# Six changes of order on four engines of a fused two-layer kernel (Trainium2, one core)

## The chip, the cores and the metric

One NeuronCore of a Trainium2 chip runs the whole kernel in one launch. The metric is the device time of one execution in microseconds (us); lower is better. The engines run side by side, each one through its own list of instructions in the order in which that list was written: TensorE (PE, matmuls, with its weight loads as PEld), VectorE (DVE), ScalarE (ACT), GpSimd (POOL) and SyncE (SP, which here only starts transfers). They wait for each other at semaphores. An instruction that waits holds up everything behind it on its engine.

## The reference

The input `x` has 4 batches of 1024 tokens with 1024 features. Four blocks follow, each with a residual and a layer norm:

```
x = layernorm(x + x @ (W0 * block_mask).T)                 # 32x32 block mask
x = layernorm(x + x @ W1.T + bias + lora(x, adapter of the batch))
x = layernorm(x + small_model(x))                          # 1024 -> 128, 4 layers, 128 -> 1024
x = layernorm(x + x @ W.T + b + routed rank-16 experts)
```

A layer of the small model is: layer norm, silu, a complex exponential scan along the sequence, residual, layer norm, 128 to 512 with silu, 512 to 128, residual. Everything is float32. The kernel gets that accuracy by splitting each factor into a high and a low part and adding three products (hi·hi, hi·lo, lo·hi).

## The kernel before, in words

The 4096 tokens are 32 tiles of 128. The first dense block works on tiles s = 0 to 31, the second on s = 32 to 63 (`A_END` = 32, `B_END` = 64), then the small model runs on 8 units of 512 tokens for each layer, and the last dense block takes s = 64 to 95. A tile has 8 chunks of features (`KC`) and two halves of 512 output columns. A product of one tile and one half is 8 chunks by 3 matmuls (`terms`), of 128x512 each.

**The pair stage.** Tiles 7 to 26 go in ten pairs p = 0 to 9 through seven half-size products in place of eight (a Strassen-like scheme). On PE they stand in the order A11, A12, S2, S3, S1, S4, A22 (`paired_product`), 12 matmuls each. ACT makes the high parts (`op_hi`), DVE the sums of x (`add_x`) and the low parts (`op_lo`). ACT copies three results from PSUM to SBUF (`hold(p, 0..2)`, for A11, S2 and S1) and DVE adds them to others (`join(p, 0..3)`). A22 of a pair waits for `join(p, 1)`, which needs `hold(p, 2)`. S1 waits for `hold(p, 1)`. After a tile's rows are joined, DVE takes the statistics (`aggregate`), POOL the reciprocal root (`root`), and ACT normalises the row (`normalise`: a small `shift`, L1410, and the row, L1413). POOL takes the row apart into two planes of 16 bits (`part_planes`), and ACT starts their transfer to a scratch tensor in device memory (`send_planes`).

**The second dense block.** Its input comes from that scratch tensor by transposing DMAs on SP's queue (`load_x`, L632, two for a tile, into `x_planes`). POOL puts the planes together into `x_in` (`join_planes`, L2640), and ACT and DVE split it into high and low (`split_x`). `x_planes` and `x_in` are one buffer each, so tile s+1 can't be fetched before tile s is joined, and not be joined before tile s is split. In tiles 27 to 31 the weights of the second block are built as well: a product on PE (`weight_part`, L979), a sum on DVE (`weight_sum`, L1932), high and low parts. `split_x(32)` stands ahead of the sums for parts 13 to 15 on both ACT and DVE.

**The last eight tiles of it (s = 56 to 63)** also carry the set-up of the small model. DVE builds tables of angles and centres weights (`prepare(j)` with j = s - 56); PE turns each finished row (`turn_y`, L1030), ACT and DVE split it (`split_y`), and a projection (`project_pair`) takes two tiles at a time to 128 features. From s = 60 on the small model's first steps begin (`EARLY` = 4): ACT squares a unit (`square1`, L1502), PE takes the variance (`variance1`, L1072), DVE copies it (`take_var1`), POOL takes the root (`root1`, L2653, turn letter "a"), PE spreads it (`spread_rstd1`, L1078), DVE scales (`scale1`), ACT applies silu (`silu_x`, L1513), then come rotation and scan. The second half of a tile's product waits until DVE has taken the tile before out of its bank (L1840).

All orders are written out by hand, in one long sequence for each engine; there is no scheduler.

Of the kernel before, what the change touches and what calls it, by code (L numbers as in the profile page):

```python
# [9 lines left out]
BATCHES = 4  # L10
# [13 lines left out]
FIRST = 3  # L24
# [15 lines left out]
A_END, B_END, D_END = TILES, 2 * TILES, 3 * TILES  # L40
# [7 lines left out]
EARLY = 4  # L48
# [194 lines left out]
def build(nc, a, out):  # L243
# [184 lines left out]
    with ExitStack() as ctx:  # L428
# [175 lines left out]
        def _(sp):  # L604
# [123 lines left out]
            for s in range(2, A_END):  # L728
# [11 lines left out]
                if s == S_END:  # L740
                    for n in range(2, 6):
                        load_w(n)
                    sp.wait_ge(mm_done, product_count(PAIRS - 1, A22))
                    sp.dma_start(a_in[:], a["expert_a"]).then_inc(lora_loaded, 16)
                    load_x(s + 3)
                if s > S_END:
                    for n in range(TAIL_PARTS[s].start + 3, min(TAIL_PARTS[s].stop + 3, PARTS)):
                        load_w(n)
                if s == S_END + 2:
                    for i in range(2):  # L750
                        sp.wait_ge(stored[(S_END - 1 - i) % 2], 16 * ((S_END - 1 - i) // 2 + 1))
                    sp.dma_start(bias1[:], a["bias1"].partition_broadcast(P)).then_inc(bias_loaded, 16)
                if s + 2 >= A_END:
                    load_x(s + 2)

            for s in range(A_END, B_END):
                b, j = batch_of(s), s % TPB
# [588 lines left out]
        def _(act):  # L1346
# [45 lines left out]
            def t_hi(m):  # L1392

                act.wait_ge(summed, KC + 1 + 2 * m + 2)
                if m >= 4:
                    act.wait_ge(w0_lo_ready, t_count(m - 2))
                act.activation(t_place(m)[:, 0], t_source(m), ACT.Identity).then_inc(w0_hi_ready, 1)
# [215 lines left out]
            normalise(3)  # L1613
            evacuate(4, 1)
            t_hi(7)
            send_planes(3)
            split_x(FIRST + 3)
            normalise(4)
            evacuate(5, 0)
            for j in range(A11, S1):  # L1620
                op_hi(0, j)
            send_planes(4)
            evacuate(5, 1)
            normalise(5)
            evacuate(6, 0)
            evacuate(6, 1)
# [3 lines left out]
            for p in range(PAIRS):  # L1630
# [6 lines left out]
                    op_hi(p + 1, A11)  # L1637
                if p > 0:
                    send_planes(a - 2)
                normalise(a - 1)  # L1640
                if more:
                    op_hi(p + 1, A12)
                else:
                    split_x(S_END)
                hold(p, 1)
                if more:
                    op_hi(p + 1, S2)
                    op_hi(p + 1, S3)
# [33 lines left out]
            for s in range(A_END, B_END):  # L1682
# [17 lines left out]
                    weight_hi(n + 1)  # L1700
                if s == A_END:
                    send_planes(s - 1)
                if s > B_END - EARLY:
                    silu_x(s - 1 - B_END + EARLY)
                if s >= B_END - EARLY:
                    square1(s - B_END + EARLY)
                if i >= 1:
                    split_y(s - 1)

# [60 lines left out]
        def _(dve):  # L1770
# [688 lines left out]
            for s in range(A_END, B_END):  # L2459
# [23 lines left out]
                if b + 1 < BATCHES:  # L2483
                    for m in range(n, n + 2):
                        weight_sum(m)
                        weight_lo(m)
                if i >= 1:
                    split_y(s - 1)
                if b + 1 == BATCHES:
                    prepare(j)  # L2490
                if s >= B_END - EARLY:
                    turn = s - B_END + EARLY
# [116 lines left out]
        def _(pool):  # L2609
# [137 lines left out]
            root(S_END - 1)  # L2747
            part_planes(S_END - 2)
            for s in range(S_END, A_END):
                for i, n in enumerate(TAIL_PARTS[s]):  # L2750
                    if n % 2:
                        weight_lo(n)
                    if i == 1 and s > S_END:
                        root(s - 1)
                part_planes(s - 1)
                if s + 2 >= A_END:
                    join_planes(s + 2)

            order = [("d", rotate_back(0)), ("d", rotate_back(1)), ("b", rotate), ("a", root1), ("e", root2)]
            root(A_END - 1)  # L2760
            part_planes(A_END - 1)
            for s in range(A_END, B_END):
                if s + 2 < B_END:
                    join_planes(s + 2)
                root(s)
                if B_END - EARLY <= s + 1 < B_END:
                    turn_of(order, s + 1 - B_END + EARLY)

# [87 lines left out]
```

## Time and profile before

| | before |
|---|---|
| time, median of 3 runs | 1662.61 us (1660.96 to 1665.57) |
| the profiled execution | 1665.42 us, span 1663.4 us |
| PE busy | 1617.6 us, 97% |
| DVE, ACT, POOL busy | 1171.7, 667.3, 615.5 us (70%, 40%, 37%) |
| mean granted TensorE clock | 0.989 |

The span is the time from the first to the last instruction; the execution's own time has about 2 us around it. PE is busy nearly all the time, so what a change of order can give lies in the time in which PE stands still, and in the time after it in which PE runs at a lower clock. PE busy is a share of modelled matmul times and hides this second part; it is seen in the granted clock of a stretch. In a row of the timeline, the bracket at the end is the idle time of that engine just before the instruction and what ended it.

### The profile page before, as it was taken

The page shows a single profiled execution, that of the slowest core. Times are in us where ns is not written, and L with a number is a line of the kernel's source. Part 1 is how long each engine was busy: PE and PEld are TensorE (multiplying, and loading weights), DVE is VectorE, ACT ScalarE, POOL GpSimd, SP SyncE. Part 2 cuts the span into 40 slices and gives each one's busy share as a digit, 9 for nine tenths or more (in the row PEclk, how much of TensorE's full clock was granted, in tenths as well). Part 3 has the DMA queues.
Part 4 walks back from the last instruction along what each step waited for, and adds up shares of the span by engine and source line. Part 5 has one row for each costly group of instructions (what it writes and reads, how often), then busy time and mean ns, then how long its engine had stood idle before and what let it go on. Part 6 is the DMA issues. An engine that isn't in the chain of part 4 may idle for free.

```text
span 1663.4 us, 22807 instructions
## 1 busy us (share of the span) xinstructions
PE 1617.6 (97%) x7734; PEld 1298.9 (78%) x7734; DVE 1171.7 (70%) x2150; ACT 667.3 (40%) x987; POOL 615.5 (37%) x507
## 2 busy tenths in 40 slices
PE   9999999999999999998899999999899999999998
PEld 7877777878888888887776676666688788888886
DVE  7878887646656565675777777778867777776633
ACT  3544444433333333322345555545533333333311
POOL 4324333443333222221477777772213212221200
PEclk9999999999999999999989999999999999999999
DMA  7233333544545444632140000002546555555421
GB/s 279 84 113 121 114 101 127 170 114 132 126 111 125 113 122 116 162 92 76 42 161 26 1 1 1 1 13 95 206 146 214 192 198 190 187 195 188 134 82 51
DMA packets 140195, 196.58 MB, mean 118 GB/s; under 512 B 75954, under 2 KB 84146, under 8 KB 139826
## 3 DMA queue, kind: packets, MB, share of 16 engines
q1 hardware_dynamic: 115250, 125.92, 25.9%
q10 hardware_dynamic: 24832, 69.22, 10.8%
q8 instruction: 63, 1.03, 0.3%
q14 instruction: 50, 0.41, 0.1%
HBM read 105.97 MB, written 72.35 MB: 107 GB/s over the span
## 4 chain that ended last, share of the span: by engine, by line
PE 75%; DVE 10%; issue 7%; POOL 3%; ACT 3%; DMA 2%; ACTq 0%; SPq 0%; POOLq 0%; DVEq 0%
PE ps L884 14%; PE ps L886 13%; PE ps L885 13%; PE ps L1130 6%; PE ps L1072 3%; PE ps L963 2%; PE ps L965 2%; PE ps L964 2%; PE ps L1030 2%; PE ps L1120 2%; PE ps L1078 2%; PE ps L1122 2%; PE ps L1121 2%; PE ps L896 2%; PE ps L1098 1%
## 5 line engine op out<-in xcount | busy, mean ns | idle before, releaser
L2622 POOL TENSOR_TENSOR rstd<-var_eps,minus_half 128x1 f32<-128x1 f32 x96 | 87.5, 911 | 562.1 <-DVE minus_mean L1908 561.9
L884 PE MATMUL ps<-wall_x,x_hi 128*128 128x512 f32 x688 | 277.0, 403 | 8.9 <-ACT wall_x L1475 3.1
L885 PE MATMUL ps<-wall_x,x_hi 128*128 128x512 f32 x688 | 271.4, 394 | 0.0
L886 PE MATMUL ps<-wall_x,x_lo 128*128 128x512 f32 x688 | 270.9, 394 | 0.0
L884 PE MATMUL ps<-wall_y,x_hi 128*128 128x512 f32 x512 | 201.9, 394 | 0.0
L885 PE MATMUL ps<-wall_y,x_hi 128*128 128x512 f32 x512 | 199.4, 389 | 0.0
L886 PE MATMUL ps<-wall_y,x_lo 128*128 128x512 f32 x512 | 199.4, 389 | 0.0
L884 PEld LDWEIGHTS ps<-wall_x,x_hi 128*128 128x128 f32 x688 | 131.1, 191 | 39.7 <-issue 5.4
L886 PEld LDWEIGHTS ps<-wall_x,x_lo 128*128 128x128 f32 x688 | 131.2, 191 | 28.6
L885 PEld LDWEIGHTS ps<-wall_x,x_hi 128*128 128x128 f32 x688 | 131.3, 191 | 25.6
L1840 DVE TENSOR_TENSOR row<-ps,bias 128x512 f32<-128x512 f32 x128 | 87.8, 686 | 86.7 <-PE ps L886 85.4
L1541 ACT ACTIVATE g<-ps,b 128x512 f32<-128x512 f32 x128 | 83.9, 679 | 123.8 <-PE ps L1122 123.4
L1130 PE MATMUL ps<-g,w 128*128 128x512 f32 x256 | 126.9, 619 | 0.0
L1843 DVE BATCH_NORM_STATS2 stats<-row 128x6 f32<-128x512 f32 x152 | 105.1, 694 | 28.8 <-ACT row L1403 24.3
L1410 ACT ACTIVATE shift<-minus_mean,rstd 128x1 f32<-128x1 f32 x96 | 28.0, 292 | 239.5 <-POOL rstd L2622 239.5
L1413 ACT ACTIVATE row<-row,shift,rstd 128x1024 f32<-128x1024 f32 x96 | 119.5, 1245 | 3.2
L886 PEld LDWEIGHTS ps<-wall_y,x_lo 128*128 128x128 f32 x512 | 96.1, 188 | 20.4
L885 PEld LDWEIGHTS ps<-wall_y,x_hi 128*128 128x128 f32 x512 | 96.2, 188 | 18.9
L884 PEld LDWEIGHTS ps<-wall_y,x_hi 128*128 128x128 f32 x512 | 96.2, 188 | 18.8
L2640 POOL COPY x_in<-x_planes 128x1024 uint16<-128x1024 uint16 x64 | 85.2, 1378 | 26.8 <-DMA x_planes<-x_scratch 26.8
L1369 ACT ACTIVATE x_hi<-ps 128x1024 fp32r<-128x1024 f32 x32 | 32.7, 1023 | 150.6 <-PE ps L896 147.6
L1072 PEld LDWEIGHTS ps<-mean_col,squares 128*128 128x128 f32 x520 | 68.1, 194 | 26.2 <-issue 12.0
(329 smaller groups left out, 3619.2 us busy)
## 6 DMA issues: line engine op xcount, KB each, us to landing
x_scratch<-row ACTq DMA_DIRECT2D x32, 512.0 KB, 2.7
x_in<-x_scratch SPq DMA_DIRECT2D x32, 512.0 KB, 3.9
out<-row ACTq DMA_DIRECT2D x32, 512.0 KB, 2.7
x_in<-in_x_t SPq DMA_DIRECT2D x29, 512.0 KB, 3.5
w_first<-in_w_t SPq DMA_DIRECT2D x56, 256.0 KB, 3.0
x_scratch<-planes_early ACTq DMA_DIRECT2D x27, 512.0 KB, 3.1
cx<-x_scratch SPq DMA_DIRECT2D x24, 512.0 KB, 4.2
x_scratch<-cx ACTq DMA_DIRECT2D x24, 512.0 KB, 3.6
```

Source lines behind the costliest of these rows:

```text
L884: pe.matmul(bank, hi[:, k], wall[:, k, 0, cols], start=(k == 0), stop=False)
L885: pe.matmul(bank, hi[:, k], wall[:, k, 1, cols], start=False, stop=False)
L886: return pe.matmul(bank, lo[:, k], wall[:, k, 0, cols], start=False, stop=(k == KC - 1))
L896: last = pe.transpose(ps_x[:, k * P:(k + 1) * P], x_in[s % 2][:, k * P:(k + 1) * P], ident[:])
L1072: last = pe.matmul(ps[:, bank, c:c + 1], squares[:, c * P:(c + 1) * P], mean_col[:], start=True, stop=True)
L1130: pe.matmul(ps[:, OUT], w2[:, FCH * (n // UNITS) + i], g[:, i], start=(i == 0), stop=(i == FCH - 1)).then_inc(o_done, 1)
L1413: act.activation(row[:, i], row[:, i], ACT.Identity, bias=shift[:, i:i + 1], scale=rstd[:, i:i + 1])\
L1541: act.activation(g[:, i], ps[:, F0 + i % 2], ACT.Silu, bias=of_layer(b1[:, :, i], n))\
L1840: dve.tensor_tensor(row[:, i, cols], ps[:, out_bank(s, half)], bias[:, cols], ALU.add)\
L1843: mark(dve.bn_stats(stats[:, i, half], row[:, i, cols]))
L2622: pool.tensor_tensor(rstd[:, i:i + 1], var_eps[:, i:i + 1], minus_half[:, 0:1], ALU.pow)\
L2640: pool.tensor_copy(halves[:, part], x_planes[:, part].rearrange("p k t -> p (k t)"))\
```

## The change

No instruction is added or taken away; the list of PE is the same. Six things move:

1. SP and POOL, tile 32: its two transposing DMAs are issued ahead of the loads of weight parts 13 to 15, and `join_planes(32)` comes ahead of the work of tile 30 on POOL.
2. ACT, start: `split_x(6)` ahead of `send_planes(3)`, and `evacuate(5, 1)` ahead of `send_planes(4)`.
3. ACT, each of the ten pairs: `hold(p, 1)` ahead of `normalise(a - 1)` and of what follows it.
4. ACT, tiles 61 to 63: `square1` ahead of `silu_x`.
5. DVE, tiles 59 to 62 (j = 3 to 6): `prepare(j)` ahead of `split_y(s - 1)`.
6. POOL, from tile 33 on: `join_planes(s + 3)` right behind `root(s)`; so it stands ahead of the small-model steps of the turn.

```diff
@@ SP
+                if s + 2 == A_END:
+                    load_x(A_END)
                 if s > S_END:
                     for n in range(TAIL_PARTS[s].start + 3, min(TAIL_PARTS[s].stop + 3, PARTS)):
                         load_w(n)
...
-                if s + 2 >= A_END:
-                    load_x(s + 2)
+            load_x(A_END + 1)
@@ ACT, start
+            split_x(FIRST + 3)
             send_planes(3)
-            split_x(FIRST + 3)
...
+            evacuate(5, 1)
             send_planes(4)
-            evacuate(5, 1)
@@ ACT, pairs
                 if p > 0:
                     send_planes(a - 2)
+                hold(p, 1)
                 normalise(a - 1)
                 if more:
                     op_hi(p + 1, A12)
                 else:
                     split_x(S_END)
-                hold(p, 1)
@@ ACT, last tiles of the second block
+                if s >= B_END - EARLY:
+                    square1(s - B_END + EARLY)
                 if s > B_END - EARLY:
                     silu_x(s - 1 - B_END + EARLY)
-                if s >= B_END - EARLY:
-                    square1(s - B_END + EARLY)
@@ DVE
+                if b + 1 == BATCHES and j >= 3:
+                    prepare(j)
                 if i >= 1:
                     split_y(s - 1)
-                if b + 1 == BATCHES:
+                if b + 1 == BATCHES and j < 3:
                     prepare(j)
@@ POOL
             for s in range(S_END, A_END):
+                if s + 2 == A_END:
+                    join_planes(A_END)
...
-                if s + 2 >= A_END:
-                    join_planes(s + 2)
+            join_planes(A_END + 1)
...
+            join_planes(A_END + 2)
             for s in range(A_END, B_END):
-                if s + 2 < B_END:
-                    join_planes(s + 2)
                 root(s)
+                if s + 3 < B_END:
+                    join_planes(s + 3)
                 if B_END - EARLY <= s + 1 < B_END:
                     turn_of(order, s + 1 - B_END + EARLY)
```

ACT in pair 2, before. `held` are the copies of A11 and then S2; the two `x_hi` are the high parts of A11 and A12 for pair 3; `shift` and `row` are the normalising of tile 10:

```order
L1390 ACTIVATE held<-ps 128x512 [waits evac_dve,mm_done]
L1383 ACTIVATE x_hi<-x_in_126 128x512 [waits mm_done,x_loaded1]
L1421 DMA x_scratch<-planes_early 128x2x1024 [waits parted]
L1410 ACTIVATE shift<-minus_mean,rstd 128x1 [waits rstd_ready,ve_ready]
L1413 ACTIVATE row<-row,shift,rstd 128x1024 [waits shift_ready]
L1383 ACTIVATE x_hi<-x_in_126 128x512 [waits mm_done,x_loaded1]
L1390 ACTIVATE held<-ps 128x512 [waits evac_dve,mm_done]
L1383 ACTIVATE sum_hi<-x_sum 128x512 [waits mm_done,x_summed] x2
```

The same place after the change (line numbers there are one higher):

```order
L1391 ACTIVATE held<-ps 128x512 [waits evac_dve,mm_done]
L1384 ACTIVATE x_hi<-x_in_126 128x512 [waits mm_done,x_loaded1]
L1422 DMA x_scratch<-planes_early 128x2x1024 [waits parted]
L1391 ACTIVATE held<-ps 128x512 [waits evac_dve,mm_done]
L1411 ACTIVATE shift<-minus_mean,rstd 128x1 [waits rstd_ready,ve_ready]
L1414 ACTIVATE row<-row,shift,rstd 128x1024 [waits shift_ready]
L1384 ACTIVATE x_hi<-x_in_126 128x512 [waits mm_done,x_loaded1]
L1384 ACTIVATE sum_hi<-x_sum 128x512 [waits mm_done,x_summed] x2
```

The copy of S2, with its wait for PE, has moved ahead of the normalising and of the high part of A12.

DVE in tile 59, before. `row` and `stats` are the first half of tile 59, `y_lo` is `split_y(58)`, then comes `prepare(3)` (from `b_68` to `table`), then the second half of tile 59:

```order
L1843 BN_STATS stats<-row 128x6 [waits evac_dve]
L1947 TENSOR_TENSOR y_lo<-ps,y_hi 128x8x128 [waits y_hi_ready]
L2073 TENSOR_TENSOR b_68<-ps,b_in 128x16 [waits bias_done,mlp_loaded]
L2060 TENSOR_SCALAR cross_wide<-table,anchor 128x512
...
L2066 SCALAR_TENSOR_TENSOR table<-table,anchor,cross_wide 128x512 x3
L1840 TENSOR_TENSOR row<-ps,bias_142 128x512 [waits stored1,mm_done,dve_done]
```

After the change:

```order
L1844 BN_STATS stats<-row 128x6 [waits evac_dve]
L2074 TENSOR_TENSOR b_68<-ps,b_in 128x16 [waits bias_done,mlp_loaded]
L2061 TENSOR_SCALAR cross_wide<-table,anchor 128x512
...
L2067 SCALAR_TENSOR_TENSOR table<-table,anchor,cross_wide 128x512 x3
L1948 TENSOR_TENSOR y_lo<-ps,y_hi 128x8x128 [waits y_hi_ready,dve_done]
L1841 TENSOR_TENSOR row<-ps,bias_142 128x512 [waits stored1,mm_done]
```

The wait for ACT's high part of y now stands behind the table work.

POOL at tiles 59 to 61, before. `x_in_126` from `x_planes` is `join_planes` (61, then 62), `rstd` is `root`, `rstd_97` is `root1`, `x_rot_178` is the first rotation:

```order
L2640 COPY x_in_126<-x_planes 128x1024 [waits lo_ready,x_loaded0]
L2640 COPY x_in_126<-x_planes 128x1024
L2622 TENSOR_TENSOR rstd<-var_eps,minus_half 128x1 [waits normed,ve_ready]
L2653 TENSOR_TENSOR rstd_97<-var_95,minus_half 128x4 [waits var1_ready]
L2640 COPY x_in_126<-x_planes 128x1024 [waits lo_ready,x_loaded0]
L2640 COPY x_in_126<-x_planes 128x1024
L2622 TENSOR_TENSOR rstd<-var_eps,minus_half 128x1 [waits normed,ve_ready]
```

After the change:

```order
L2643 COPY x_in_126<-x_planes 128x1024 [waits lo_ready,x_loaded0]
L2643 COPY x_in_126<-x_planes 128x1024
L2625 TENSOR_TENSOR rstd<-var_eps,minus_half 128x1 [waits normed,ve_ready]
L2643 COPY x_in_126<-x_planes 128x1024 [waits lo_ready,x_loaded0]
L2643 COPY x_in_126<-x_planes 128x1024
L2656 TENSOR_TENSOR rstd_97<-var_95,minus_half 128x4 [waits var1_ready]
L2625 TENSOR_TENSOR rstd<-var_eps,minus_half 128x1 [waits normed,ve_ready]
```

The join of tile 62 no longer stands behind `root1(0)`.

## Rows read from the trace of the kernel before

**Rows 1.** Waits of PE: line and tile, releaser, us in total, times, longest.
```profile
PE ps L1072 <- ACT squares L1502: 6.0, 3, 2.8
PE ps L963 <- ACT held L1390: 5.1, 5, 1.6
PE ps L1078 <- POOL rstd L2653: 2.4, 3, 1.1
```

**Rows 2.** Stretches: length, busy us of PE, PEld, DVE, ACT, POOL; PE clock, DMA share, GB/s.
```profile
349.00:358.00 9.00, 5.78 (x19) 4.36 (x18) 5.87 (x9) 4.86 (x7) 2.72 (x4) 0.81 0.45 117
756.00:764.00 8.00, 5.93 (x20) 4.67 (x20) 5.58 (x11) 2.17 (x3) 1.52 (x1) 0.79 0.09 34
781.00:791.00 10.00, 7.16 (x34) 5.73 (x33) 4.60 (x8) 3.87 (x5) 1.27 (x1) 0.83 0.36 111
800.00:808.00 8.00, 5.96 (x28) 5.08 (x27) 6.25 (x6) 2.36 (x3) 1.33 (x1) 0.79 0.16 66
245.00:254.00 9.00, 7.28 (x32) 5.43 (x31) 7.64 (x11) 5.21 (x9) 2.48 (x2) 1.00 0.27 80
```

**Rows 3.** Timeline at tile 32: start, length, engine, line, what, idle before.
```profile
329.56 0.38 SPq L752 DMA_DIRECT2D bias<-in_bias  x1
340.58 11.18 SPq L632 DMA_TRANSPOSE x_planes<-x_scratch  x4
346.53 0.14 DVE L1908 TENSOR_SCALAR minus_mean<-mean_var 128x1 f32<-128x1 f32 x1
346.55 2.60 POOL L2640 COPY x_in<-x_planes 128x1024 uint16<-128x1024 uint16 x2 [2.22 <-DMA x_planes<-x_scratch]
350.27 1.23 DVE L1823 TENSOR_TENSOR x_lo<-x_in,x_hi 128x1024 fp32r<-128x1024 f32 x1 [3.60 <-ACT x_hi L1369]
352.57 0.67 PE L979 MATMUL ps<-b_rows,a_rows 128*128 128x512 f32 x1 [3.22 <-DVE w_first L1932]
```

**Rows 4.** Timeline of tiles 59 to 61.
```profile
751.68 1.22 DVE L1947 TENSOR_TENSOR y_lo<-ps,y_hi 128x1024 fp32r<-128x1024 f32 x1 [4.09 <-ACT y_hi L1481]
757.38 0.69 DVE L1840 TENSOR_TENSOR row<-ps,bias 128x512 f32<-128x512 f32 x1
758.12 0.50 PE L884 MATMUL ps<-wall_x,x_hi 128*128 128x512 f32 x1 [2.07 <-DVE row L1840]
774.17 1.02 POOL L2653 TENSOR_TENSOR rstd<-var,minus_half 128x4 f32<-128x4 f32 x1 [13.34 <-DVE var L2120]
775.13 2.60 POOL L2640 COPY x_in<-x_planes 128x1024 uint16<-128x1024 uint16 x2
777.77 1.06 ACT L1369 ACTIVATE x_hi<-x_in 128x1024 fp32r<-128x1024 f32 x1 [9.50 <-POOL x_in L2640]
802.62 1.34 PE L1072 MATMUL ps<-mean_col,squares 128*128 128x1 f32 x8 [2.04 <-ACT squares L1502]
```

**Rows 5.** Timeline of the start.
```profile
84.39 0.47 PE L884 MATMUL ps<-wall_x,x_hi 128*128 128x512 f32 x1 [1.57 <-issue]
```

**Rows 6.** Timeline of pairs 2 and 5, by engine.
```profile
143.05 0.29 ACT L1410 ACTIVATE shift<-minus_mean,rstd 128x1 f32<-128x1 f32 x1 [2.35 <-POOL rstd L2622]
144.49 0.39 PE L963 MATMUL ps<-wall_y,sum_hi 128*128 128x512 f32 x1
196.17 0.39 PE L963 MATMUL ps<-wall_x,x_hi 128*128 128x512 f32 x1
196.37 0.60 ACT L1390 ACTIVATE held<-ps 128x512 f32<-128x512 f32 x1 [0.33 <-PE ps L965]
198.89 0.39 PE L963 MATMUL ps<-wall_y,sum_hi 128*128 128x512 f32 x1
202.96 0.29 ACT L1410 ACTIVATE shift<-minus_mean,rstd 128x1 f32<-128x1 f32 x1 [5.46 <-POOL rstd L2622]
210.66 0.69 DVE L1893 TENSOR_TENSOR row<-ps,held 128x512 f32<-128x512 f32 x1
211.50 0.47 PE L963 MATMUL ps<-wall_y,x_hi 128*128 128x512 f32 x1
```

## The prediction, made blind

> **What bounds the kernel now.** I read the page's busy shares first: PE works 97% of the span, so the time is the matmuls' own time, the stops of PE, and the slow stretches of its clock. Next the list of PE's waits [rows 1]: no wait is large, and three lines touched by the change stand in it. L1072 waits for ACT's squares (6.0 us in three stops), L963 for a held block (5.1 us in five, the longest 1.6), and L1078 for the root `rstd` (2.4 us in three, the longest 1.1). Two more stand in the timelines: 3.22 us at tile 32 [rows 3] and 2.07 us at tile 59 [rows 4].
>
> Then I read the granted clock around these stops [rows 2]. In 349 to 358, after the stop of 3.22, it is 0.81, in 756 to 764 (a stop of 2.07) 0.79, in 781 to 791 (2.8, the longest of L1072) 0.83, and in 800 to 808 (2.04) 0.79. The level between the ends can only be a mixture of 2.4 and 1.2 GHz, so the missing share is time lost: 9 × 0.19 = 1.71, 8 × 0.21 = 1.68, 10 × 0.17 = 1.70, 8 × 0.21 = 1.68. Every stop of 2.04 us or more thus costs 1.7 us beyond itself. In 245 to 254, which holds a stop of 1.6 us for a held block, the clock stays at 1.00. Where the price begins between 1.6 and 2.04 us these rows don't tell.
>
> **Tile 32 (part 1 of the change).** The transposes are issued at 340.58 and the join begins at 346.55, 5.97 us later [rows 3]. After the change they stand behind the bias load, whose issue is at 329.56, ahead of three weight loads. Issued at about 330 they have landed at about 336; the data that they fetch was sent tiles before. The join of 2.60 us then runs about 336.6 to 339.2, seven microseconds early. What is late next is not the join but DVE: its statistics stand ahead of its part of the split and end at 346.53 + 0.14 = 346.67. So `x_lo` can go from 350.27 to about 346.7 and, with it, the sum behind it on which PE stopped: 3.5 us, against a stop of 3.22. It goes whole, with a margin of only 0.3 us, and its slow stretch with it: 3.22 + 1.7 = **−4.9 us**. POOL does the join in an idle time and its other work starts at most half a microsecond late; the three weight loads leave SP about 1 us later and are needed a tile or more later. Both I cost at nothing; uncovered, each is at most its own delay, 1 us. If the transposes gain nothing, this term is 0; if only the stop shrinks below 2 us, it is about −1.7 − 1.2.
>
> **Tiles 59 to 63 (parts 4 to 6).** At tile 59 DVE is idle for 4.09 us until ACT's high part of y is there, and starts `y_lo` at 751.68; then `prepare(3)` runs, and the second half row comes at 757.38 for 0.69, for which PE waits till 758.12 [rows 4]. `y_lo` takes 1.22, so the table work is 757.38 − 751.68 − 1.22 = 4.5 us long. With `prepare(3)` ahead it fills the 4.09 of idleness, ends about 752.2, `y_lo` follows to 753.4 and the row comes at about 754 rather than 757.4. The stop of 2.07 goes with its slow stretch: −3.8. The price is `y_lo` some half to one microsecond late; the projection that needs it is a tile away. At tile 60 POOL idles 13.34 us in front of the first unit's root, because that root waits for DVE's copy of the variance, and the join of tile 62 stands behind it, at 775.13. ACT's high part of tile 62 therefore waits 9.50 us, till 777.77. After the change the join stands behind `root(59)`, and can run about 18 us earlier; ACT's split comes ten or more earlier, and everything behind it on ACT, the squares of the second unit above all, is no longer late. Further the squares stand ahead of the silu and its table load (part 4). So I take the 2.8 us stop of L1072 as gone with its slow stretch (−4.5), the 1.1 at L1078 (−1.1) and the 2.04 at 802.62 with its slow stretch (−3.7). The sum is 3.8 + 4.5 + 1.1 + 3.7 = **−13.1 us**. What can be late next is `split_y`, now behind the table work: 4.5 us of work moved ahead of it against 4.09 of idleness leaves half a microsecond of lateness at tile 59; where DVE has less idleness, at most the full 4.5 late. The bounds of this term are 0 (all becomes other waits) and −15.
>
> **Start (part 2).** The stop of 1.57 us at 84.39 has "issue" for its releaser [rows 5]; the high parts it really waits for stand on ACT behind a transfer's start, itself waiting for POOL. The change takes them out of that queue. But the next A22 products wait for DVE's chain below, so of 1.57 us I keep only about 0.35 by pair 1; 0 to 1.6 are the bounds.
>
> **Pairs (part 3).** The held block is now ahead of the normalising on ACT. Before, at pair 5, the normalising starts at 202.96, as soon as POOL's root is there, and the copy comes after it. A product is 198.89 − 196.17 = 2.72 us on PE [rows 6], and a copy starts 0.20 after the next product's first matmul (196.37 − 196.17) and takes 0.60. So from now on the normalising, N, can't start before S3's start + 0.80. What follows N sets A22: shift, row, the high part of A12, DVE's low parts and sums and `join(p, 1)` at 210.66, then A22 at 211.50: 211.50 − 202.96 = 8.54 us. From S3's start to A22 PE itself needs three products, 8.16 us. A22 thus waits 0.80 + 8.54 − 8.16 = 1.18 us in a pair that had no wait, and a pair takes 7 × 2.72 + 1.18 = 20.22 us in place of 19.04. In pair 2, N was at 143.05 and S3 at 144.49. Less 0.35 from the start, plus 0.80, N comes at 144.94: 1.9 late. Between there and pair 5's N the trace has 59.91 us for three pairs, 19.97 each, since there were waits already. If pair 5's intervals become 20.22 flat, the lateness grows by 0.75 only; if each grows by the full 1.18, by 3.5. That gives 2.6 to 5.4 us at pair 5; I take 4.2, and no more after it, since there the held block was waited for already. That wait (5.1 us in all) goes from the list but gains nothing: S1 starts earlier, and A22 still waits for the 8.54 us chain from N. It moves from S1 to A22, and there the two waits meet: 1.18 plus up to 1.6 is 2.8 us in one piece, above the 2.04 after which the clock was seen to fall. I take two such falls of 1.7. The term is 4.2 + 3.4 = **+7.6 us**. Below, it can be −5 (the waits of 5.1 just go); above, see the third rival.
>
> **Sum.** −4.9 − 13.1 + 7.6 = −10.4 us. The profiled execution took 1665.42 us, 2.1 us of it around the span of 1663.4; −10.4 makes 1655.0. It lay 2.8 us above the median of 1662.61, to which the same step gives 1652.2. I forecast **1652 us**. A difference below 0.3%, 5 us, can't be told from no change here.
>
> **Rivals.**
> *The held block costs nothing.* If the chain behind N has slack that I don't see (DVE's row work could be started by an earlier root), A22 keeps its time and the first gains stay: −4.9 − 13.1 and a little of the start, up to −1.6: 1643 to 1645 us. For it: most pairs show no wait of PE at S1, and the wait list has 5.1 us to gain. Against it: 8.54 > 8.16 in pair 5. Chance 26%.
>
> *The released waits only change their name.* In tiles 59 to 63 the late `split_y` (up to 4.5 us) and the late DVE work behind it take the place of the roots and squares; half of 13.1 comes back, and the pair term stays: −4.9 − 6.5 + 7.6 = −3.8, 1659 us. For it: DVE is busy 70% of the time and 6.25 of 8 us in 800 to 808 [rows 2]; against it: it had 4.09 idle at tile 59. Chance 14%. Of this kind, that the transposes at tile 32 land late because the change of SP's queue doesn't bring them forward: −13.1 + 7.6 = −5.5, 1657 us; chance 5%, as 5.97 us from issue to join leaves ten microseconds of room.
>
> *The clock falls in every pair (the other side).* The merged or lengthened wait at A22 need only be a little longer than I have it (above about 2 us instead of 1.18) for a slow stretch in each pair. A pair then takes 20.22 + 1.7 = 21.9 us against 19.97, times nine intervals, 17.6, and 1.9 from the first: +19.5 − 18.0 = +1.5, 1664 us; with waits of 2 us in each, 8 more, 1672 us. It decides if the wait at A22 passes the 1.6 to 2.04 us between which the fall begins. Chance 8%. Here the Trainium skill speaks against the change: "TensorE: Matmul & The Clock Gate", section "HAM oscillation — how this bites in real kernels", says that waits that come back between bursts of matmuls throw the clock back to half in each tile anew. By that rule alone this rival's 1664 would be the forecast; the trace before agrees only for stops of 2.04 us and more, and its 1.6 us stops in the pairs left the clock at 1.00.
>
> **How the numbers follow.** My forecast 47%, the held block free 26%, half the tail gain 14%, transposes late 5%, clock in every pair 8%. The range: downward to the first rival with half a microsecond, 1642.5; upward through 1657 and 1659 to 1660; beyond it lies the last rival and the rest of the scatter. Faster by over 0.3% (below 1657.6): the forecast, the first rival and part of the others, 0.81; within 0.3%: 0.13; slower: 0.06.
>
> **What would show it.** In the list of waits: the held block at L963 near 0 and about 10 us for DVE's row or `x_hi` at L963 new; no stop over 2 us at tile 32, nor before 758, 784 and 802; L1072's 6.0 down to about 1. In the timeline: the join of tile 32 seven, of tile 62 eighteen us earlier in its tile; N in the pairs 0.80 behind S3's start. In the windows: 1.00 at tiles 32 and 59 to 62, and two places below 1.00 in the pairs. The forecast is wrong if the time from tile 7 to tile 26 does not grow, or if the tail's waits return as waits for `y_lo` or the angle tables.

## The result, and the profile after

| | before | after |
|---|---|---|
| median of 5 runs | 1665.57 us (1660.96 to 1668.10) | 1655.73 us (1653.47 to 1656.24) |
| the profiled execution's span | 1663.4 us | 1654.3 us |
| PE busy | 1617.6 us | 1614.8 us |

The ratio is 0.9942 with a 95% interval of 0.9922 to 0.9962: 9.8 us faster between the medians of the same chip, where the forecast had 10.4. The median of 1655.73 lies inside the forecast's range of 1642.5 to 1660 and 3.7 us above its 1652. Of these, 3.0 are no error of a step: the forecast counted down from the earlier median of 1662.61, and the runs made beside the changed kernel put the kernel before at 1665.57.

To see where the time went, I take fixed points of the program in both timelines: the normalising of tiles 7, 26, 57 and 65 (the ACT instruction `shift`), and PE's first stop for squares of the next layer (at 890.70 us before, 878.88 after). The table gives how much each stretch grew against before. The first stretch contains the launch and the first loads; its length differs by up to 2 us either way between executions (−2.1 to +1.8 in the table of the experiments).

| stretch | growth | forecast |
|---|---|---|
| launch to tile 7 (start, most of pair 0) | +1.0 | in the pairs' term |
| tile 7 to 26 (pairs) | +7.0 | +7.6 |
| 26 to 57 (tile 32) | −5.0 | −4.9 |
| 57 to the stop at 890.70 | −14.9 | −13.1 |
| from there to tile 65 (small model) | +2.9 | 0 |

PE's waits in the changed kernel, in the columns of [rows 1]; line numbers are one to three higher:

```profile
PE ps L964 <- DVE row L1894: 12.1, 9, 2.3
PE ps L1073 <- ACT squares L1503: 1.1, 1, 1.1
PE ps L999 <- ACT b_rows L1438: 0.9, 1, 0.9
PE ps L1079 <- POOL rstd L2656: 0.8, 2, 0.6
PE ps L980 <- DVE w_first L1933: 0.7, 1, 0.7
PE ps L885 <- DVE row L1841: 0.7, 2, 0.5
```

The 5.1 us for a held block are gone, and nine waits of the same product family for a joined row, 12.1 us, stand in their place. The squares went from 6.0 to 1.1 us. A stop of 0.9 us for `b_rows`, at the end of the pairs, is new and I had not foreseen it.

The windows, in the columns of [rows 2]: the first three are the places of tile 32 and of tiles 59 to 61 in this run's time, the other three hold the A22 stops of pairs 1, 5 and 7.

```profile
357.00:366.00 9.00, 9.00 (x41) 7.38 (x41) 5.28 (x10) 4.70 (x8) 5.98 (x6) 1.00 0.17 59
759.00:767.00 8.00, 8.00 (x46) 6.88 (x45) 7.93 (x13) 3.18 (x5) 4.32 (x3) 1.00 0.36 110
773.00:783.00 10.00, 10.00 (x61) 8.82 (x61) 4.74 (x7) 4.91 (x7) 2.86 (x3) 1.00 0.26 93
130.00:140.00 10.00, 7.79 (x28) 5.96 (x27) 9.66 (x28) 5.08 (x8) 1.05 (x2) 0.83 0.47 159
216.00:225.00 9.00, 6.67 (x30) 5.45 (x30) 8.40 (x26) 4.93 (x9) 1.81 (x3) 1.00 0.36 117
258.00:267.00 9.00, 7.00 (x31) 5.74 (x31) 8.52 (x30) 4.51 (x9) 2.13 (x3) 1.00 0.39 120
```

The first three are the places of three of the stops in [rows 2]. PE is now busy for all of each stretch, at full clock. In the pairs one window, at 130 to 140, shows 0.83: 10 × 0.17 = 1.7 us lost. I had expected two of those.

Timeline of pair 4 in the changed kernel, beside [rows 6]; start, length, engine, line, what:

```profile
187.57 0.39 PE L964 MATMUL ps<-wall_y,sum_hi 128*128 128x512 f32 x1
187.77 0.60 ACT L1391 ACTIVATE held<-ps 128x512 f32<-128x512 f32 x1 [4.02 <-PE ps L966]
188.26 0.28 ACT L1411 ACTIVATE shift<-minus_mean,rstd 128x1 f32<-128x1 f32 x1
189.73 0.61 ACT L1384 ACTIVATE x_hi<-x_in 128x512 fp32r<-128x512 f32 x1
190.38 1.09 DVE L1851 TENSOR_TENSOR x_lo<-x_in,x_hi 128x512 fp32r<-128x512 f32 x1 [3.47 <-ACT x_hi L1384]
195.97 0.69 DVE L1894 TENSOR_TENSOR row<-ps,held 128x512 f32<-128x512 f32 x1
196.80 0.47 PE L964 MATMUL ps<-wall_y,x_hi 128*128 128x512 f32 x1 [0.91 <-DVE row L1894]
```

This is the chain that the prediction described. S3 starts at 187.57, the copy 0.20 later, the normalising 0.49 after that: 0.69 behind S3's start, where I had 0.80. From the normalising to A22 it is 196.80 − 188.26 = 8.54 us, the same as before. The idle time of DVE is the new thing here: it waits 3.47 us for the high part of A12, which stands behind the copy and the normalising on ACT.

In pair 5, one of the three with a long stop, the copy is not what the normalising waits for. The copy starts at 208.00 and takes 0.60; the normalising comes 2.1 us behind S3's start, with POOL's root:

```profile
209.91 0.29 ACT L1411 ACTIVATE shift<-minus_mean,rstd 128x1 f32<-128x1 f32 x1 [1.31 <-POOL rstd L2625]
```

From it to A22 at 218.44 it is again 8.53 us. The normalising waits for the later of the two, the copy or the root.

Timeline at tile 32, beside [rows 3]:

```profile
338.10 4.03 SPq L632 DMA_TRANSPOSE x_planes<-x_scratch  x2
344.69 2.66 POOL L2643 COPY x_in<-x_planes 128x1024 uint16<-128x1024 uint16 x2 [2.96 <-DVE x_lo L1824]
354.86 1.23 DVE L1824 TENSOR_TENSOR x_lo<-x_in,x_hi 128x1024 fp32r<-128x1024 f32 x1
355.69 0.39 PE L980 MATMUL ps<-b_rows,a_rows 128*128 128x512 f32 x1
```

The join came 6.6 us behind the transposes here, and its idle time was ended by DVE's split of tile 31 rather than by the transfer, so the data had landed before. DVE's `x_lo` follows its statistics with no idle time, as forecast, and PE's product on the sums has no stop.

Timeline of tiles 59 and 60, beside [rows 4]:

```profile
756.07 1.22 DVE L1948 TENSOR_TENSOR y_lo<-ps,y_hi 128x1024 fp32r<-128x1024 f32 x1
757.21 0.68 DVE L1841 TENSOR_TENSOR row<-ps,bias 128x512 f32<-128x512 f32 x1
760.61 2.84 POOL L2643 COPY x_in<-x_planes 128x1024 uint16<-128x1024 uint16 x2
768.48 0.15 DVE L2121 TENSOR_SCALAR var<-ps 128x4 f32<-128x4 f32 x1
768.72 1.02 POOL L2656 TENSOR_TENSOR rstd<-var,minus_half 128x4 f32<-128x4 f32 x1 [5.26 <-DVE var L2121]
```

At tile 58 this execution runs 2.7 us behind the one before (749.50 against 746.77). The half row at 757.21 is therefore at 754.5 in the old time; the forecast said about 754. The join of tile 62 is at 760.61, in old time 757.9, 17 us earlier than 775.13. The copy of the variance is at 768.48, in old time 765.8; before, it ended an idle time of POOL at 774.17 [rows 4].

### The profile page after: what moved, and what is told of

Read it like the earlier page. It is cut to its first block, busy times and chain, and to the rows that moved or that the text cites. A ratio compares the mean times of both kernels' runs of the same rounds, so it can differ in the third digit from the quotient of the medians.

```text
span 1654.3 us, 22809 instructions
## 1 busy us (share of the span) xinstructions
PE 1614.8 (98%) x7734; PEld 1299.1 (79%) x7734; DVE 1175.0 (71%) x2150; ACT 666.4 (40%) x987; POOL 618.5 (37%) x507
## 4 chain that ended last, share of the span: by engine, by line
PE 78%; DVE 10%; issue 5%; ACT 3%; DMA 2%; POOL 1%; ACTq 0%; SPq 0%; DVEq 0%; POOLq 0%
PE ps L885 15%; PE ps L887 14%; PE ps L886 14%; PE ps L1131 7%; PE ps L1073 3%; PE ps L1031 2%; PE ps L1079 2%; PE ps L1123 2%; PE ps L964 2%; PE ps L1121 2%; PE ps L1122 2%; PE ps L897 2%; PE ps L966 2%; PE ps L965 2%; PE ps L1099 1%
## 5 line engine op out<-in xcount | busy, mean ns | idle before, releaser
L885 PE MATMUL ps<-wall_x,x_hi 128*128 128x512 f32 x688 | 273.8, 398 | 4.9 <-ACT wall_x L1476 2.1
L886 PE MATMUL ps<-wall_x,x_hi 128*128 128x512 f32 x688 | 268.8, 391 | 0.0
L2636 POOL COPY planes_early<-row 128x1024 uint16<-128x1024 uint16 x54 | 65.9, 1249 | 61.2 <-ACT row L1414 48.1
```

What stands on the lines that cost most here:

```text
L885: pe.matmul(bank, hi[:, k], wall[:, k, 0, cols], start=(k == 0), stop=False)
L886: pe.matmul(bank, hi[:, k], wall[:, k, 1, cols], start=False, stop=False)
L2636: pool.tensor_copy(planes[s >= S_END][:, part], halves[:, part]).then_inc(parted, 1)
```

## The experiments

All medians of one group share the runs of the kernel before on their chip. Growth of each stretch against before, in us, from the profiled executions, with the same fixed points as above:

| kernel | median (before) | to 7 | 7–26 | 26–57 | 57–stop | to 65 |
|---|---|---|---|---|---|---|
| changed | 1655.73 (1665.57) | +1.0 | +7.0 | −5.0 | −14.9 | +2.9 |
| hold_only | 1674.42 (1664.77) | +1.8 | +8.4 | 0.0 | +4.2 | −0.5 |
| hold_back | 1646.10 (1664.77) | −1.0 | −0.3 | −3.6 | −13.8 | −1.1 |
| high_first | 1641.17 (1664.77) | −1.1 | −5.2 | −4.4 | −13.7 | +3.1 |
| high_first_hold_last | 1639.95 (1664.77) | −1.6 | −5.1 | −4.7 | −13.8 | −1.1 |
| tile32_only | 1660.82 (1665.23) | +1.2 | −0.1 | −5.2 | +0.2 | −0.6 |
| table_only | 1654.11 (1665.23) | −1.0 | −0.1 | −0.6 | −12.8 | −1.4 |
| joins_only | 1660.08 (1665.23) | +1.0 | 0.0 | −2.7 | −2.6 | −0.6 |
| joins_squares | 1657.54 (1665.23) | +0.3 | 0.0 | −1.3 | −4.4 | −0.7 |
| best_again | 1641.19 (1666.83) | −2.1 | −5.2 | −5.4 | −12.5 | +2.8 |
| best_no_joins_squares | 1644.01 (1666.83) | −0.7 | −5.2 | −4.7 | −13.5 | +2.8 |
| best_no_table | 1646.00 (1666.83) | −0.8 | −5.2 | −3.6 | −6.7 | −0.4 |
| best_old_start | 1642.20 (1666.83) | +0.1 | −5.2 | −3.7 | −14.1 | −1.2 |

high_first_hold_last and best_again are one kernel: in the last column they differ by 3.9, in the one before by 1.3. The first and the last column carry such scatter; the column of the pairs does not. The column to the stop carries it too: hold_only has +4.2 there, though its edit ends at tile 26 and its stops in these tiles are those of the kernel before. The clock settles it. After nearly equal stops (2.04 before, 2.06 in hold_only) the low stretch was twice as long here; 10 × 0.34 = 3.4 us lost, against 1.7 in [rows 2]:

```profile
812.00:822.00 10.00, 7.94 (x29) 6.80 (x29) 8.06 (x7) 2.36 (x3) 1.33 (x1) 0.66 0.12 50
```

So a difference of 1 to 4 us in one execution's last two columns needs its stops and its clock beside it before it says anything of an edit.

**hold_back**: the held block at its old place.

```diff
-                hold(p, 1)
                 normalise(a - 1)
                 if more:
                     op_hi(p + 1, A12)
                 else:
                     split_x(S_END)
+                hold(p, 1)
```

> The changed kernel with the held block behind the normalising and the high part of A12 again, as it was before; all else as changed. My theory (the early copy delays the high part of A12 on ACT, DVE's x_lo waits 2.7 to 3.9 us for it, and A22 waits for the join behind it): the nine waits of A22 for a joined row (12.1 us) go, the five waits for the held block (5.1 us) come back, and so does the clock of the pairs; 7 to 8 us faster than the changed kernel, about 1648. Rival (the held block costs nothing, the 7 us that tiles 7 to 27 lost are from the new order at the start): stays at 1655 or gets 5 us slower.

Measured: 1646.10 (1644.74 to 1646.97), ratio to before 0.9888 (0.9871 to 0.9905). Its interval doesn't touch that of the changed kernel, and it is 9.6 us faster by the medians, a little more than the 7 to 8 expected. PE's waits in it:

```profile
PE ps L964 <- ACT held L1391: 4.9, 5, 1.6
```

The nine waits for a joined row are gone, the stretch of the pairs is back to −0.3. The rival is out.

**hold_only**: the same edit alone, on the kernel before.

```diff
+                hold(p, 1)
                 normalise(a - 1)
                 if more:
                     op_hi(p + 1, A12)
                 else:
                     split_x(S_END)
-                hold(p, 1)
```

> The kernel before with only the held block moved ahead of the normalising in the ten pairs. My theory: slower by 6 to 8 us, 1671 beside 1664; nine waits of A22, 0.9 us each where the pair had none and 2.0 to 2.3 where the held block was waited for. Rival: 5 us faster, since the wait list loses 5.1 us.

Measured: 1674.42, ratio 1.0059 (1.0043 to 1.0076), slower by 9.7 us between the medians, where I expected 6 to 8. The profiled execution was the slowest of the six, 1679.38 us, and its +8.4 in the pairs is the part that the edit made; the +4.2 of the last eight tiles is the clock's, as shown above. The wait and two windows of its pairs, at the stops of pairs 1 and 5:

```profile
PE ps L963 <- DVE row L1893: 11.9, 9, 2.3
```

```profile
130.00:140.00 10.00, 7.80 (x28) 5.98 (x27) 9.73 (x25) 4.24 (x8) 1.89 (x2) 0.83 0.46 159
217.00:226.00 9.00, 6.78 (x23) 5.45 (x24) 8.40 (x26) 3.91 (x7) 2.04 (x3) 0.81 0.36 117
```

Here the clock fell twice, as the prediction had it (9 × 0.19 = 1.7), where the changed kernel showed one fall in the same pairs at nearly equal stops (2.34 and 2.33 us in pair 5). One fall is 1.7 us, near the 1.4 between +8.4 and +7.0.

**high_first**: the high part of A12 ahead of both.

```diff
-                hold(p, 1)
-                normalise(a - 1)
                 if more:
                     op_hi(p + 1, A12)
                 else:
                     split_x(S_END)
+                hold(p, 1)
+                normalise(a - 1)
```

> The changed kernel with the high part of A12 of the next pair ahead of both the held block and the normalising on ACT. If the cost is that this high part stands behind the normalising (my theory), DVE's x_lo of A12 starts as soon as DVE is free, at least 1.3 us earlier also in the pairs where the normalising waits for its root; the 0.9 us waits of A22 go, those of 2.0 to 2.3 shrink to 1 or less, the held block isn't waited for: 10 to 12 us faster than the changed kernel, about 1645, and faster than hold_back. Rival (A22's chain runs through the normalised row itself, which is now 0.6 us later still): the waits of A22 stay or grow, 1656 or more.

Measured: 1641.17, ratio 0.9858 (0.9842 to 0.9875). PE's waits, and DVE's low part of A12 in pair 4, in its timeline:

```profile
PE ps L964 <- DVE row L1894: 1.7, 3, 0.9
```

```profile
179.20 0.68 DVE L1851 TENSOR_TENSOR x_lo<-x_in,x_hi 128x512 fp32r<-128x512 f32 x1
179.79 0.69 DVE L1872 TENSOR_TENSOR x_sum<-x_in 128x512 f32<-128x512 f32 x1
```

The 12.1 us have shrunk to 1.7. DVE no longer waits for the high part. The held block and the normalising stand in the same order as in the changed kernel, so it is neither of them by itself that costs. The low part takes 0.68 us now, not 1.09: in the changed kernel POOL's copy of planes ran beside it (189.89 to 192.37), here POOL does nothing from 178.04 to 182.70. The gain over the changed kernel is 14.6 us by the medians, more than the 10 to 12 expected; 12.2 of it is in the pairs. Against hold_back the intervals just overlap (0.9875 and 0.9871); the pairs' −5.2 against −0.3 tells the two apart.

**high_first_hold_last**: as above, but the normalising ahead of the held block.

```diff
                 if more:
                     op_hi(p + 1, A12)
                 else:
                     split_x(S_END)
-                hold(p, 1)
                 normalise(a - 1)
+                hold(p, 1)
```

> The changed kernel with the order high part of A12, normalising, held block. By my theory the order of these two is worth little once the high part stands ahead of both: the normalising is not held up by PE, the held block is late only where its root is, by about 0.6 us less than before the change: waits of S1 of 0 to 1 us in five pairs, 2.5 in all, which A22's chain would not have let PE use before. About 1646 to 1648. If the held block's place were what costs, this would equal hold_back.

Measured: 1639.95 (1639.12 to 1640.48), ratio 0.9850 (0.9837 to 0.9864), the fastest version, and a median of 1641.19 when it was run again. I had expected 1646 to 1648. The waits of S1 came to 2.1 us, near the 2.5 expected, but they stand in place of A22's waits, of which none is left, and do not add to them. It can't be told from high_first; the interval of hold_back, 0.9871 to 0.9905, lies above it.

**tile32_only**: on the kernel before, the transposes and the join of tile 32 moved (part 1 of the change).

```diff
+                if s + 2 == A_END:
+                    load_x(A_END)
...
+                if s + 2 == A_END:
+                    join_planes(A_END)
```

> The kernel before with only the change at tile 32 on SP and POOL. Theory: the stop of 3.2 us before the product on the sums goes and the clock stays at 1.00 in the stretch behind it: 4.9 us faster. Rival (the clock's fall there has another cause than the stop): 3.2 us faster, with a stretch below 1.00 left.

Measured: 1660.82, ratio 0.9972 (0.9960 to 0.9985); 4.4 us between medians, −5.2 in the stretch. The interval allows 2.5 to 6.7 us, so the times alone leave both 4.9 and 3.2. The trace decides: of the two stops for `w_first`, 3.9 us together before, the one of 3.22 is gone, and the stretch behind its place runs at full clock:

```profile
PE ps L980 <- DVE w_first L1933: 0.7, 1, 0.7
350.00:359.00 9.00, 9.00 (x41) 7.47 (x41) 5.31 (x11) 4.75 (x9) 6.19 (x6) 1.00 0.17 62
```

**table_only**: on the kernel before, `prepare(j)` ahead of `split_y` for j ≥ 3 (part 5).

```diff
+                if b + 1 == BATCHES and j >= 3:
+                    prepare(j)
                 if i >= 1:
                     split_y(s - 1)
-                if b + 1 == BATCHES:
+                if b + 1 == BATCHES and j < 3:
                     prepare(j)
```

> The kernel before with only the table work ahead of the split of y on DVE at tiles 59 to 62. Theory: the stop of 2.1 us at tile 59 goes with its slow stretch, 3.8 us faster there; the stops for the squares stay, since they hang on the join of tile 62 behind the first root. Rival (released only into a wait for the split y): less than 2 us.

Measured: 1654.11, ratio 0.9928 (0.9901 to 0.9954), and −12.8 in its stretch. Both theories fall: it frees nearly all. The waits, and DVE and POOL around the first root in its timeline; the last line is DVE's split of y at tile 60 in the kernel before:

```profile
PE ps L1072 <- ACT squares L1502: 1.9, 2, 1.1
PE ps L1078 <- POOL rstd L2655: 1.3, 2, 0.7
```

```profile
762.52 1.23 DVE L1947 TENSOR_TENSOR y_lo<-ps,y_hi 128x1024 fp32r<-128x1024 f32 x1 [0.99 <-ACT y_hi L1481]
763.66 0.15 DVE L2120 TENSOR_SCALAR var<-ps 128x4 f32<-128x4 f32 x1
763.89 1.02 POOL L2655 TENSOR_TENSOR rstd<-var,minus_half 128x4 f32<-128x4 f32 x1 [7.76 <-DVE var L2120]
764.86 2.61 POOL L2642 COPY x_in<-x_planes 128x1024 uint16<-128x1024 uint16 x2
```

```profile
768.30 1.23 DVE L1947 TENSOR_TENSOR y_lo<-ps,y_hi 128x1024 fp32r<-128x1024 f32 x1 [6.55 <-ACT y_hi L1481]
```

The join of tile 62 still stands behind the first root, as in [rows 4], but that root runs at 763.89 in place of 774.17, because DVE's copy of the variance is ten microseconds earlier. On DVE it stands behind `y_lo` and the table work in both kernels. But before, DVE idled 6.55 us for ACT's high part and only then did `y_lo` and 4.5 us of table work; now the table work fills the idle time and 0.99 of it is left. The ten are 1.8 us by which this whole execution is ahead at tile 58, 3.8 for the stop of tile 59 with its slow stretch, and the 4.5 of the table work. With the root the join is ten microseconds earlier too.

**joins_only**: on the kernel before, the joins moved from tile 33 on (part 6).

```diff
+            join_planes(A_END + 2)
             for s in range(A_END, B_END):
-                if s + 2 < B_END:
-                    join_planes(s + 2)
                 root(s)
+                if s + 3 < B_END:
+                    join_planes(s + 3)
```

> The kernel before with only the joins moved right behind the roots from tile 33 on. Theory: the join of tile 62 comes 15 us or more earlier, ACT's split with it; the stop of 2.8 us for the squares goes or shrinks to 1 with its slow stretch, and the later one of 2.0 perhaps: 4 to 8 us faster. The stop of 2.1 at tile 59 stays. Rival (the squares are late for ACT's own order, behind the silu): the stops stay, within 1 us of before.

Measured: 1660.08, ratio 0.9967 (0.9954 to 0.9980), and −2.6 in its stretch. Its waits:

```profile
PE ps L1078 <- POOL rstd L2653: 4.0, 3, 2.7
PE ps L1072 <- ACT squares L1502: 2.8, 2, 1.7
PE ps L884 <- DVE row L1840: 2.7, 3, 2.1
```

By the medians that is 5.2 us, inside the 4 to 8 expected, but it isn't where I expected it: only 2.6 us are in the last eight tiles, and 2.7 are in the stretch from tile 26 to 57, where the stop at tile 32 was 2.49 us in this execution (2.53 in joins_squares) and no fall followed it. The squares' 6.0 us went to 2.8, but the spread of the root's 2.4 went to 4.0. One stop was taken, and the next wait on the same chain grew: the root waits for DVE's variance, which comes at 773.47, as late as before. This is the second rival of the prediction, in a kernel where this edit stands alone.

**joins_squares**: part 4 added to it.

```diff
+                if s >= B_END - EARLY:
+                    square1(s - B_END + EARLY)
                 if s > B_END - EARLY:
                     silu_x(s - 1 - B_END + EARLY)
-                if s >= B_END - EARLY:
-                    square1(s - B_END + EARLY)
```

> The kernel before with the joins behind the roots from tile 33 on and the squares ahead of the silu. Theory: 1 to 3 us faster than the joins alone, since the stop at the second and later units' squares then goes whole and with it its slow stretch: 7 to 9 us faster than before. If the joins alone have taken both stops already, equal to the joins alone.

Measured: 1657.54, ratio 0.9961 (0.9940 to 0.9983), −4.4 in its stretch: 1.8 more than the joins alone by the profile; by the intervals the two are not told apart. The medians' 7.7 us are in the 7 to 9 expected, the 4.4 in its stretch are not. The spread of the root still waits 4.0 us.

**Four runs of the fastest kernel**: once as it is, and with one part taken back in each of the three others. Their edits are the ones shown above (parts 4 and 6; part 2; part 5), reversed.

> The kernel with the high part of A12 first, then the normalising, then the held block, and all else as changed, once more beside its variants: 1640, as a measure for the three others.

> The same with the joins and the squares back in their old places; the table work stays ahead of the split of y. My prediction gave 9.3 of the 13.1 us of the last eight tiles to stops that the joins and squares free. If that holds, this is 5 to 9 us slower, 1645 to 1649. Rival, from the run with the table work alone (only one stop of 0.8 us was left in those tiles): the stops all hung on DVE, and this is within 1 us, 1640 to 1641.

> The same with ACT's start as before. Theory (the gain of the start was hidden behind DVE's chain in pair 0 only because the pairs were bound by it; with the pairs freed it is kept): the stop of 1.3 to 1.6 us at 84 comes back, 1 to 1.6 us slower. Rival (the start is followed by a wait of the same length at S2's low part): no difference.

> The same with the table work behind the split of y again, joins and squares as changed. By the rival of the run without joins and squares this is where the tail's gain sits: a stop of 2.1 at tile 59 and one of 2.7 at the first root's spread, each with its slow stretch of 1.7: 8 to 9 us slower, 1648. By my prediction's terms: 3.8 us slower, 1644.

Measured, as ratios to before: best_again 0.9845 (0.9830 to 0.9860), best_no_joins_squares 0.9858 (0.9841 to 0.9874), best_old_start 0.9855 (0.9838 to 0.9872), best_no_table 0.9875 (0.9852 to 0.9899). By the medians the joins and squares are worth 2.8 us, the start 1.0, the table work 4.8; the intervals of the four overlap, so the profile's stretches must decide. Expected were 5 to 9 us or at most 1 for joins and squares, 1 to 1.6 for the start, and 8 to 9 or 3.8 for the table work; only the start came out as expected. There the part from tile 57 to the stop is −12.5 with everything (−13.8 in the other execution of this kernel), −13.5 without joins and squares, and −6.7 without the table work. So, once the table work stands ahead, joins and squares add nothing there that this measure shows, and without it they reach half. The 8 to 9 us were not reached because of the clock: the two stops that I expected are both back in best_no_table, 2.07 us at 748.54 and 2.67 us at 781.74, but only the first was followed by a fall. Its window behind the second:

```profile
779.00:789.00 10.00, 7.33 (x42) 6.29 (x42) 9.79 (x16) 2.88 (x4) 4.21 (x3) 1.00 0.13 52
```

The start: 84.53 is where the stop of 1.77 us comes back in best_old_start,

```profile
84.53 0.47 PE L885 MATMUL ps<-wall_x,x_hi 128*128 128x512 f32 x1 [1.77 <-issue]
```

and its row of tile 7 stands 0.8 to 2.2 us later than in the three others. That fits a gain of about 1, within the launch's scatter.

## Why the prediction was right, point by point

**The sum.** −9.8 us between the medians against −10.4, and the mechanisms of tile 32, of the pairs and of tile 59 were the ones described. That the sum came this near is luck in part. In the profile the last eight tiles gave 1.8 us more than forecast, the pairs' sum hides two errors of opposite sign, and the small model shows +2.9 that no term had.

**Tile 32.** Right in size and in cause: −5.0 in the changed kernel and −5.2 with this part alone, against −4.9; −3.6 to −5.4 over all nine kernels that have it. The stop of 3.22 us and its slow stretch went together.

**The start.** The stop of 1.57 us went. I kept 0.35 of it by pair 1. In the changed kernel A22 of pair 0 waits 0.91 us for a joined row and starts 0.12 us later than before, so the gain was spent there; when the pairs are freed it is worth about 1 us.

**The pairs.** The recurrence came out by its parts: 8.54 us from the normalising to A22, 20.23 us for a pair (from A22 at 176.57 to A22 at 196.80) where I had 20.22. Against before, A22 is 0.98 us late in pair 1, 3.69 in pair 2, 1.2 more in each of pairs 3 and 4, 6.95 in pair 5, and no later than that up to pair 8, as forecast. Two terms were mis-sized, and their errors nearly cancel. The clock fell once, not twice: 1.7 in place of 3.4. The waits made more: without that fall the lateness is 5.2 us at pair 5 and 6.3 at the end, where I had 4.2 for both. The last 1.1 is pair 9, where no wait for a held block stood before and which I left out. Together that is the +8.0 of the table's first two stretches, against +7.6. I also had the three long stops as a sum, 1.18 plus up to 1.6; they measured 2.0 to 2.3, because the normalising waits for the later of copy and root and not for one after the other. Two falls were seen in the kernel with this edit alone. The first rival, that the held block costs nothing, is refuted by hold_back and hold_only: 7.3 and 8.4 us in the stretch of the pairs. I had given it 26%. One reason that I gave for it was misread: PE waits at S1 in five of the ten pairs [rows 1], so not "most" are without a wait.

**What the pairs' step offered and I didn't see.** The chain behind the normalising contained the high part of A12 only because it stands behind it in ACT's list. I priced this chain as fixed. Moving that one instruction ahead took 12 us from the pairs (−5.2 against +7.0).

**The last eight tiles.** The sum was near (−13.1 against −14.9), and the four stops that I listed are all gone in the changed kernel; the split among the edits was wrong. I gave 3.8 to the table work and 9.3 to joins and squares. The runs show the reverse: table work alone −12.8, joins alone −2.6, joins and squares −4.4. The step that failed is the cause of the squares' gain: "the join of tile 62 stands behind it", behind the first unit's root, and so moving the join frees the squares. It did run 17 us earlier, but the root's own wait, 13.34 us for DVE's variance in [rows 4], was behind it: that copy came after 6.55 us of idle DVE and then 4.5 us of table work. Both edits act on this one chain, so their gains don't add: −12.8 and −4.4 make 17.2, and together they gave 14.9. This column's scatter is of the size of the difference; that the table work alone gives −13.5 where all three give −12.5 and −13.8 is the stronger evidence. In the sum it didn't show, because all three were made.

**The second and third rivals.** That released waits only change their name was true for the joins by themselves. That the clock falls in every pair was not: of the nine stops, six are of 0.9 to 1.1 us, and one of the nine was followed by a fall. The Trainium skill's rule on the oscillating clock ("TensorE: Matmul & The Clock Gate", section "HAM oscillation — how this bites in real kernels") tells of waits that come back between bursts and slow each tile anew, in a kernel whose waits it gives as about 3 to 5 us. The nine here are 0.9 to 2.3 us, so it did not speak for 1664 us as I had it; in this trace the clock did not fall tile by tile.

**What I missed.** The 0.9 us stop for `b_rows` at the end of the pairs. It is there in the two kernels with the held block ahead of a high part that is still behind the normalising (changed, hold_only), and not in hold_back or high_first; which instruction it hangs on was not tried, but the timeline shows it. The last pair has no next A12; in its place `split_x(27)` stands behind the normalising, and behind that comes the copy `b_rows`, for which PE waits until 295.29:

```profile
294.66 0.57 ACT L1438 ACTIVATE b_rows<-ps 128x512 fp32r<-128x512 f32 x1
```

Before the change this copy was made at 285.43.

## What to carry to other kernels

When a wait on one engine is moved up its list, look at what now stands behind it, and at who reads that: here a 0.6 us copy that waited for PE held up a 0.6 us instruction that DVE needed. When several stops lie on one chain, name the instruction that is late first and price its edit alone; gains of edits on one chain don't add. And if a chain between two points comes out fixed, ask which of its links is there by data and which only by the order of a list.

## What the runs showed of the hardware

A stop of 2 us or more doesn't always bring the clock down, as I had read from [rows 2]. In the pairs, after 2.21 us (pair 1) it was 0.83 in the window; after 2.33 (pair 5) and 2.00 (pair 7) it stayed at 1.00, while in hold_only 2.34 us in pair 5 gave 0.81. The longest stops that no fall followed are 2.67 us in best_no_table (its window is above) and 2.49 us at tile 32 in joins_only, whose window is the first line below. And the clock also fell where no stop of even 0.4 us stands in the nine microseconds before: the second line is from the kernel before, where PE is busy for 7.78 of 8 us.

```profile
350.00:359.00 9.00, 6.52 (x29) 5.43 (x30) 6.60 (x10) 3.96 (x7) 3.65 (x4) 1.00 0.43 117
726.00:734.00 8.00, 7.78 (x33) 6.31 (x33) 4.69 (x10) 1.54 (x2) 4.08 (x3) 0.79 0.42 139
```

A fall cost 1.7 us in the pairs, at tile 32 and in the windows of [rows 2], but 3.4 in hold_only's window of 812 to 822. So "every stop of 2.04 us or more costs 1.7 us" held for the four stops it was read from and not in general; as a price per stop it is an average at best. What decides these runs don't show.

DVE's x_lo of 128x512 takes 0.68 us, and 1.09 us while POOL copies planes; the sum behind it 0.69 and 1.52 (213.05 us in the changed kernel, POOL's copies running from 211.54 to 214.02):

```profile
213.05 1.52 DVE L1872 TENSOR_TENSOR x_sum<-x_in 128x512 f32<-128x512 f32 x1
```

The same kernel's profiled execution differs by 3.9 us in the small model between two runs. Its clock tells why: in best_again it is 0.62 from 1148 to 1166 us, 18 × 0.38 = 6.8 us lost, and in high_first_hold_last 0.79 from 1155 to 1163, 1.7 lost. A difference of that size in one profile's last stretch says nothing of an edit.
